# Cross-attention on one core: statistics two pairs ahead in a shared bank, squares on ScalarE, normalisation as two tensor products

## The reference

```python
mu  = mean(x, axis=(1, 2)); var = var(x, axis=(1, 2))      # one pair of numbers a sample
xn  = (x - mu) * rsqrt(var + 1e-5) * gamma + beta
q   = Wq xn + bq;  k, v = split(Wkv ctx + bkv)             # 8 heads of 64
att = softmax(q k^T / 8)                                   # 256 x 256 for each head and sample
out = x + Wo concat(att v) + bo
```

## Time and profile before

| | us |
|---|---|
| median of 3 runs | 746.16 (744.21 to 749.26) |
| the profiled execution | 746.77 |
| its span, first to last instruction | 744.9 |
| busy in it: PE, DVE, ACT, POOL | 675.6, 690.6, 623.1, 579.6 |
| granted TensorE clock, mean | 0.998 |

### The profile page before, as it was taken

How to read it: one execution, slowest core, us unless ns; L and a number is a source line. 1 busy time by engine, 2 the same in 40 slices (tenths; PEclk the granted TensorE clock), 3 DMA queues, 4 the chain that set the end, 5 groups by cost and what they waited for, 6 DMA issues and landing times.

```text
span 744.9 us, 29909 instructions
## 1 busy us (share of the span) xinstructions
PE 675.6 (91%) x11204; PEld 447.4 (60%) x11204; DVE 690.6 (93%) x1124; ACT 623.1 (84%) x2248; POOL 579.6 (78%) x360
## 2 busy tenths in 40 slices
PE   5889989999999999999999999999999999999986
PEld 4556566566666656666656666665666665666654
DVE  1589999999999999999999999999999999999993
ACT  2579888888988889888888998888988888898883
POOL 2477978777888777898877788877789888788873
PEclk9999999999999999999999999999999999999999
DMA  6022222222222222222222221222221222222111
GB/s 120 19 53 74 53 59 72 70 69 74 64 55 62 69 67 70 78 50 59 67 69 68 75 69 45 68 68 68 70 78 51 58 67 69 73 76 58 45 44 32
DMA packets 74814, 47.56 MB, mean 64 GB/s; under 512 B 33748, under 2 KB 74708, under 8 KB 74772
## 3 DMA queue, kind: packets, MB, share of 16 engines
q1 hardware_dynamic: 72848, 46.59, 23.6%
q10 hardware_dynamic: 1924, 0.40, 0.3%
HBM read 25.96 MB, written 4.19 MB: 40 GB/s over the span
## 4 chain that ended last, share of the span: by engine, by line
PE 57%; DVE 23%; issue 12%; ACT 4%; SPq 2%; DMA 1%; DVEq 0%; ACTq 0%
PE z L400 32%; PE fill L366 20%; DVE neg_max L537 9%; DVE probs_t L550 8%; ACT probs L482 3%; PE z L411 3%; DVE squared L580 3%; SPq L291 1%; DMA wv<-in_L_xattn_Wkv 1%; DVE recip L543 1%; DVE y L593 1%; PE z L421 1%; DVE variance L586 1%; DMA x<-in_x 1%; PE z L378 1%
## 5 line engine op out<-in xcount | busy, mean ns | idle before, releaser
L638 POOL TENSOR_TENSOR probs<-probs,recip 128x1024 f32<-128x1024 f32 x256 | 482.0, 1892 | 131.3 <-DVE recip L543 127.1
L482 ACT ACTIVATE probs<-fill,neg_max 128x256 f32<-128x256 f32 x1024 | 473.2, 484 | 92.1 <-DVE neg_max L537 88.8
L537 DVE TENSOR_REDUCE neg_max<-fill 128x4 f32<-128x1024 f32 x256 | 306.7, 1208 | 15.5 <-PE fill L366 15.2
L366 PE MATMUL fill<-c,t 64*128 64x256 f32 x2048 | 289.1, 407 | 32.0 <-ACT probs L482 28.6
L550 DVE STREAM_TRANSPOSE probs_t<-probs 128x1024 f32<-128x1024 f32 x256 | 311.5, 1222 | 0.8 <-POOL probs L638 0.8
L400 PE MATMUL z<-probs_t,ctx_keys 32*64 32x256 f32 x8192 | 254.4, 381 | 12.2 <-DVE variance L586 10.9
L366 PEld LDWEIGHTS fill<-c,t 64*128 64x128 f32 x2048 | 183.2, 190 | 125.4 <-ACT probs L482 95.7
L400 PEld LDWEIGHTS z<-probs_t,ctx_keys 32*64 32x64 f32 x8192 | 176.5, 131 | 77.2 <-issue 35.7
L482 ACT ACTIVATION_READ_ACCUMULATOR probs<-fill,neg_max 128x1 f32 x1024 | 221.7, 216 | 0.0
L491 ACT ACTIVATE t<-z,d_col 128x512 f32<-128x512 f32 x128 | 88.5, 741 | 7.1 <-PE z L378 7.0
L652 POOL TENSOR_SCALAR xhat<-x,mean,rstd 128x256 f32<-128x256 f32 x64 | 78.1, 1221 | 0.1
(11 more groups left out here) (38 smaller groups left out, 109.8 us busy)
## 6 DMA issues: line engine op xcount, KB each, us to landing
ctx_keys<-ctx_turned SPq DMA_DIRECT2D x512, 32.0 KB, 1.8
x<-in_x SPq DMA_DIRECT2D x64, 128.0 KB, 2.7
c<-in_ctx SPq DMA_DIRECT2D x64, 128.0 KB, 2.7
ctx_rows<-in_ctx SPq DMA_DIRECT2D x128, 32.0 KB, 1.7
x_res<-in_x SPq DMA_DIRECT2D x32, 128.0 KB, 2.1
out<-y SPq DMA_DIRECT2D x32, 128.0 KB, 1.7
wq<-in_L_xattn_Wq ACTq DMA_DIRECT2D x2, 128.0 KB
wv<-in_L_xattn_Wkv SPq DMA_DIRECT2D x2, 128.0 KB
```

What stands on the lines that cost most here:

```text
L366: mm = pe.matmul(banks[:, o, K * qt:K * qt + K], t[p][r:r + 64, hp, s, 128 * qt:128 * qt + 128], c2[p][r:r + 64, s, :], start=True, stop=True)
L482: ins = act.activation(probs[:, k % SLOTS, g, :], bank[:, K * qt:K * qt + K], ACT.Exp, bias=neg_max[:, k, g:g + 1], accum_out=denom[:, k, ...
L537: dve.tensor_reduce(neg_max[:, k, :], fill[k % PAIRS_OF_BANKS][:, :, :].rearrange("p o (t k) -> p (o t) k", t=QT), AX.X, ALU.max, negate=T ...
L638: pool.tensor_tensor(p, p, recip[:, k, :].unsqueeze(2).broadcast_to([128, 2 * QT, K]), ALU.mult).then_inc(probs_ready, 1)
```

## The change

The statistics are computed earlier and in other pieces. The channel moments belong to the pair three ahead, the mean to the pair two ahead, the variance to the pair ahead. `channel_spread` becomes `centre` (DVE) and `squares` (ACT: each of two columns times itself by the scale operand); PE adds squares and channel variances by two matmul calls into one sum. POOL subtracts the mean from both samples at once in place, and later multiplies both by the inverse root. `mean_var` and `mean` have two buffers. All five order tables are new. The diff without the new buffers' declarations and the branches that call the new functions:

```diff
-PE_ORDER = (at('scores', 0.00, 1.12, 3.45, 4.98, 7.20, 10.10, 10.87, 13.52)
-            + at('mix', 18.00, 18.76, 20.22, 21.75, 22.51, 23.96, 24.73, 25.42) + at('project_out', 30.21)
-            + at('project_in', -4.44, -3.75) + at('mean', -16.22) + at('var', -15.24))
-ACT_ORDER = (at('exp', 1.93, 3.39, 5.57, 7.31, 9.13, 12.04, 13.84, 15.63) + at('t', -2.59, -0.79, 1.00, 1.43)
-             + at('z', 26.50, 27.24))
-DVE_ORDER = (at('weights', -2.64, 0.96) + at('max', 0.98, 2.44, 4.61, 6.36, 8.18, 11.09, 11.92, 14.52)
-             + at('recip', 4.28, 6.30, 8.04, 9.87, 10.78, 13.60, 15.35, 18.38)
-             + at('turn', 7.19, 9.01, 9.93, 12.75, 13.66, 15.41, 19.42, 21.45) + at('moments', -30.11)
-             + at('mean_var', -28.73) + at('spread', -15.74) + at('sample_var', -14.19)
-             + at('turn_context', 4.34) + at('result', 32.64))
-POOL_ORDER = (at('divide', 5.51, 6.92, 8.33, 10.63, 12.04, 13.80, 15.54, 18.58) + at('root', -12.01)
-              + at('norm', -10.47, -6.26))
-SYNC_ORDER = (at('load_x', -5.06) + at('load_c', 14.52) + at('load_ct', 5.14) + at('spread_context', 4.94)
-              + at('residual', 24.64) + at('store', 33.14))
+PE_ORDER = (at('scores', 0.00, 1.50, 3.83, 5.37, 7.58, 10.49, 11.25, 13.91)
+            + at('mix', 18.38, 19.14, 20.59, 22.13, 22.90, 24.35, 25.11, 25.80) + at('project_out', 30.59)
+            + at('project_in', -4.06, -3.37) + at('mean', -31.26) + at('var', -15.24))
+ACT_ORDER = (at('exp', 2.24, 3.89, 6.01, 7.76, 9.52, 12.42, 14.22, 16.01) + at('t', -2.21, -0.41, 1.38, 1.81)
+             + at('z', 26.89, 27.62) + at('square', -22.87))
+DVE_ORDER = (at('weights', -2.26, 1.34) + at('max', 0.98, 2.93, 5.05, 6.81, 8.56, 11.47, 12.87, 14.81)
+             + at('recip', 4.99, 6.75, 8.50, 9.40, 12.81, 14.74, 15.70, 19.77)
+             + at('turn', 7.64, 9.46, 10.35, 13.88, 15.76, 18.07, 20.13, 21.89) + at('moments', -35.70)
+             + at('mean_var', -34.29) + at('centre', -30.20) + at('sample_var', -14.18)
+             + at('turn_context', 3.83) + at('result', 32.62))
+POOL_ORDER = (at('divide', 6.07, 7.47, 8.88, 10.29, 13.01, 14.93, 17.03, 19.96) + at('root', -13.56)
+              + at('norm', -15.66, -10.63))
+SYNC_ORDER = (at('load_x', -9.43) + at('load_c', 14.91) + at('load_ct', 4.63) + at('spread_context', 4.43)
+              + at('residual', 24.62) + at('store', 33.12))
...
                     if kind == "load_x" and owner.shift(2).exists():
-                        wait(sync, xhat_ready, owner.count(PS, PS))
+                        wait(sync, xhat_ready, owner.count(1, 1))
                         load_x(owner.shift(2), rows[kind])
...
+                    if pair.shift(3).exists():
+                        wait(pe, centred_ready, pair.shift(3).count(2, 2))
...
             def sum_means(pair):
                 wait(pe, mean_var_ready, pair.count(PS, PS))
                 if pair.shift(-1).exists():
-                    wait(pe, t_ready, pair.shift(-1).count(HP, 2))
+                    wait(pe, centred_ready, pair.shift(-1).count(2, 2))
+                if pair.shift(-2).exists():
+                    wait(pe, variance_ready, pair.shift(-2).count(1, 1))
+                    wait(pe, t_ready, pair.shift(-2).count(HP, 2))
+                pe.matmul(z[:, 1, 0:PS], ones[:, :], mean_var[pair.parity()][:, :, 0], start=True, stop=True
+                          ).then_inc(mean_summed, 1)
+
+            def sum_spreads(pair):
+                wait(pe, squared_ready, pair.count(PS, PS))
                 if pair.shift(-1).exists():
                     wait(pe, variance_ready, pair.shift(-1).count(1, 1))
-                pe.matmul(z[:, 1, 0:PS], ones[:, :], mean_var[:, :, 0], start=True, stop=True).then_inc(mean_summed, 1)
-
-            def sum_spreads(pair):
-                wait(pe, spread_ready, pair.count(1, 1))
-                pe.matmul(z[:, 1, PS:2 * PS], ones[:, :], spread[:, :], start=True, stop=True).then_inc(var_summed, 1)
+                    wait(pe, t_ready, pair.shift(-1).count(HP, 2))
+                pe.matmul(z[:, 1, PS:2 * PS], ones[:, :], squared[:, :], start=True, stop=False)
+                pe.matmul(z[:, 1, PS:2 * PS], ones[:, :], mean_var[pair.parity()][:, :, 1], start=False, stop=True
+                          ).then_inc(var_summed, 1)
...
+            def squares(pair):
+                wait(act, centred_ready, pair.count(2, 2))
+                for s in range(PS):
+                    act.activation(squared[:, s:s + 1], centred[:, s:s + 1], ACT.Identity, scale=centred[:, s:s + 1]
+                                   ).then_inc(squared_ready, 1)
...
-            def channel_spread(pair):
+            def centre(pair):
+                p = pair.parity()
                 wait(dve, mean_summed, pair.count(1, 1))
                 if pair.shift(-1).exists():
-                    wait(dve, xhat_ready, pair.shift(-1).count(PS, PS))
-                dve.tensor_copy(mean[:, :], z[:, 1, 0:PS]).then_inc(centred_ready, 1)
-                dve.tensor_tensor(centred[:, :], mean_var[:, :, 0], z[:, 1, 0:PS], ALU.subtract
+                    wait(dve, var_summed, pair.shift(-1).count(1, 1))
+                if pair.shift(-2).exists():
+                    wait(dve, xhat_ready, pair.shift(-2).count(1, 1))
+                dve.tensor_copy(mean[p][:, :], z[:, 1, 0:PS]).then_inc(centred_ready, 1)
+                dve.tensor_tensor(centred[:, :], mean_var[p][:, :, 0], z[:, 1, 0:PS], ALU.subtract
                                   ).then_inc(centred_ready, 1)
-                wait(dve, centred_ready, pair.count(2, 2))
-                dve.tensor_tensor(squared[:, :], centred[:, :], centred[:, :], ALU.mult).then_inc(squared_ready, 1)
-                wait(dve, squared_ready, pair.count(1, 1))
-                dve.tensor_tensor(spread[:, :], squared[:, :], mean_var[:, :, 1], ALU.add).then_inc(spread_ready, 1)
...
             def inverse_root(pair):
-
                 wait(pool, variance_ready, pair.count(1, 1))
-                wait(pool, x_loaded[pair.parity()], pair.dma_count(1) * 2)
                 if pair.shift(-1).exists():
-                    wait(pool, xhat_ready, pair.shift(-1).count(PS, PS))
+                    wait(pool, xhat_ready, pair.shift(-1).count(1, 1))
+                pool.tensor_tensor(rstd[:, :], variance[:, :], minus_half[:, :], ALU.pow).then_inc(rstd_ready, 1)
+
+            def subtract_mean(pair):
+                p = pair.parity()
+                wait(pool, centred_ready, pair.count(2, 2))
+                wait(pool, x_loaded[p], pair.dma_count(1) * 2)
+                pool.tensor_tensor(x2[p][:, :, :], x2[p][:, :, :], mean[p][:, :].unsqueeze(2).broadcast_to([128, PS, S]),
+                                   ALU.subtract).then_inc(x_centred, 1)
+
+            def normalise(pair):
+                p = pair.parity()
+                wait(pool, x_centred, pair.count(1, 1))
+                wait(pool, rstd_ready, pair.count(1, 1))
+                if pair.shift(-1).exists():
                     wait(pool, projected, pair.shift(-1).count(HP // 2, HP // 2))
-                pool.tensor_tensor(rstd[:, :], variance[:, :], minus_half[:, :], ALU.pow).then_inc(rstd_ready, 1)
-
-            def normalise(pair, s):
-                p = pair.parity()
-                pool.tensor_scalar(xhat[:, s, :], x2[p][:, s, :], mean[:, s:s + 1], rstd[:, s:s + 1],
-                                   ALU.subtract, ALU.mult).then_inc(xhat_ready, 1)
+                pool.tensor_tensor(xhat[:, :, :], x2[p][:, :, :], rstd[:, :].unsqueeze(2).broadcast_to([128, PS, S]),
+                                   ALU.mult).then_inc(xhat_ready, 1)
```

More of the change, by code:

```diff
@@ L162, in build @@
         moments = sb("moments", [128, PS, 6])
-        mean_var = sb("mean_var", [128, PS, 2])
-        mean = sb("mean", [128, PS])
+        mean_var = [sb(f"mean_var_{i}", [128, PS, 2]) for i in range(2)]
+        mean = [sb(f"mean_{i}", [128, PS]) for i in range(2)]
         centred = sb("centred", [128, PS])
         squared = sb("squared", [128, PS])
-        spread = sb("spread", [128, PS])
         variance = sb("variance", [128, PS])
@@ L201, in build @@
         squared_ready = sem("squared_ready")
-        spread_ready = sem("spread_ready")
         var_summed = sem("var_summed")
@@ L205, in build @@
         rstd_ready = sem("rstd_ready")
+        x_centred = sem("x_centred")
         xhat_ready = sem("xhat_ready")
@@ L371, in project_in @@
                 if i == 0:
-                    wait(pe, xhat_ready, pair.count(PS, PS))
+                    wait(pe, xhat_ready, pair.count(1, 1))
                 if pair.shift(-2).exists():
@@ L511, in steps @@
                         exponentials(owner, item)
+                    elif kind == "square":
+                        squares(owner)
                     else:
@@ L569, in channel_mean_var @@
                 for s in range(PS):
-                    dve.bn_aggr(mean_var[:, s, :], moments[:, s, :]).then_inc(mean_var_ready, 1)
```

(22 more changed lines are left out.)

## The result

| | before | changed |
|---|---|---|
| median of 6 runs, us | 746.25 | 915.33 (911.07 to 918.78) |
| ratio | | 1.226, 95% interval 1.222 to 1.231 |
| profiled execution, its span, us | 746.77, 744.9 | 918.57, 916.8 |
| granted TensorE clock, mean | 0.998 | 0.879 |

What follows compares the result with a forecast made beforehand. DVE was taken to set the pace, PE close behind; after the change DVE waits on SP's queue for x. Start 37.2, 28 periods of 26.7 (747.6), 101.3 after, 1.9 around: 888 us, range 868 to 935.

Steps and rivals of the forecast that it cites:

- first project_in starts: PE's start: waiting for the early statistics and later loads, project_in begins near 22.6 us in place of 14.87.
- first context turn: DVE's first turn_context, delayed by the later start and the extra matmul, from 28.86 to about 37.2 us.
- SP's leg: From turn_context's end to x in place: 12.49 us of queue, 0.75 to second issue, 2.9 to land; 16.1 us.
- moments to the turn's end: DVE's work from x's landing to the next turn_context's end, with nothing else late: 10.6 us.
- period: Distance between successive pairs' context turns: 10.6 + 16.1 = 26.7 us against 22.02.
- last turn of 28 to the end: From pair 28's context turn to the end: 95.6 us before, plus one last stall of 5.7, makes 101.3.
- rival D: At the moments of P+3: x is there in time, 21.4 us a pair, 736 us; chance 0.06.
- the likeliest case: DVE stalls for x behind SP's queue, clock at full speed: 888 us; chance 0.53.
- Rival B: PE's idle time during the stall lowers the clock: 1.1 us more a period, 919 us; chance 0.30.
- the stall: DVE reaches moments before x has landed and stands still 5.7 us, from P = 0 to P = 28.
- ACT's squares: Two 128x1 squares on ACT at 0.25 us each, 0.5 a pair (0.4 to 1.0), hidden in idle time.
- POOL's products: POOL's normalisation as two tensor_tensor over 512, about 0.95 us each, 1.9 in all; worth nothing on the path.

Runs made afterwards that it cites:

- Experiments 1: Changed kernel with load_x moved ahead of the four load_ct transfers in SP's order, behind spread_context; 833.01 us, 1.114 to the kernel before.
- Experiment 2: Changed kernel with load_x moved ahead of spread_context in SP's order; 796.63 us, 1.067 to the kernel before.
- experiment 3: Changed kernel with load_x ahead of spread_context and the residual's load ahead of both in SP's order; 735.63 us, 0.985 to the kernel before.
- experiment 5: Changed kernel with project_out's sixteen matmul calls done three times in all but the last pairs; 891.13 us, 1.193 to the kernel before.
- experiment 4: Changed kernel with DVE's moments moved after the pair's last turn and mean_var behind the result; 819.30 us, 1.097 to the kernel before.
- experiment 7: Kernel before with squared and spread formed by one DVE tensor_scalar per sample instead of two tensor_tensor; 731.84 us, 0.980.

## Why the prediction was right, and where it was short

The prediction's steps, in the changed kernel's profiled execution:

| step | forecast, us | measured, us |
|---|---|---|
| first project_in starts | 22.6 | 22.56 |
| first context turn | 37.2 | 36.48 |
| turn's end to moments (SP's leg) | 16.1 | 16.25 in the pair shown, 16.52 as a mean of 28 |
| moments to the turn's end | 10.6 | 11.4 with the clock down, 10.45 without, 11.13 as a mean of 28 |
| period | 26.7 | 27.65 |
| last turn of 28 to the end | 101.3 | 106.2 |
| span | 886.1 | 916.8 |

**Right, and shown:** the place, the reason and the price of SP's leg. Experiments 1, 2 and 3 take it away in steps (period 27.65, 24.68, 23.54, 21.44), and the last brings the time that rival D named. The start was right to 0.1 us for project_in. The forecast's 37.2 for the first context turn is 0.3 us more than its own terms give (28.86 + 7.73 + 0.35 = 36.9).

**Short by 30.7 us of span**: 26.5 in the 28 periods (774.1 against 747.6), 4.9 after them, 0.7 less at the start. Two terms of the period were mis-sized. The second leg, 10.6 us, measured 11.13: in the likeliest case the forecast kept the clock at full speed, and with it up the leg measures 10.24 to 10.45, so the clock is the whole of this error and a little more. SP's leg, 16.1 us, measured 16.52: in most pairs it was 16.0 to 16.6, but 17.4 to 18.9 in pairs 1 to 4 and 18.1 in pair 27, where the issues were dearer than in the pair from which the forecast took them. Rival B is what happened: it forecast 1.1 us a pair more and an idle PE of 4.7 us; with PE kept busy 0.84 us came back (experiment 5), and the idle time was 3.44 us. Its sum, 919, came close to the profiled 918.57 with some luck, since it knew nothing of the dearer issues and of the tail. I gave it 0.30 beside 0.53; the trace of before had one fall, after a stretch with PE busy for 1.56 of 4 us, and the stall made sparser ones (0.95 us busy from 416 to 420), with a fall in every pair. Weighing the tail's 2.43 us of idleness against it was the mistake. The Trainium skill, TensorE: Matmul & The Clock Gate, section Why this matters for your kernels, spoke for B with its warning of idle gaps, and the trace agrees for the gap of 3.44 us.

**SP's dearer issues.** In pairs 1 to 4, and from 27 on, the same sixteen issues take longer, in some of these pairs the four of `load_ct` too:

```profile
782.37 11.11 SPq L290 DMA_DIRECT2D ctx_keys<-ctx_turned  x16
...
811.04 11.05 SPq L290 DMA_DIRECT2D ctx_keys<-ctx_turned  x16
822.14 2.59 SPq L253 DMA_DIRECT2D ctx_rows<-in_ctx  x4
```

11.05 and 2.59 us in place of 10.13 and 1.95. Most of the sixteen still follow each other at 0.63 us; one of them takes 1.57 (at 817.36), and one of the four 1.16. The kernel before has that too (11.60 at 76.51), but there it was hidden. Pairs 0 to 2 and those from 27 on are written out, and 3 and 4 are the loop's first pass; but pair 0 was at 10.09 us. What makes these issues dear wasn't tried.

**The 4.9 us after the periods** are SP's only in part. The last context turn is at 882.83 and the end 33.97 us later; before, the turn is at 713.51 and the end 31.39 later. These 2.6 us stand in the kernel of experiment 3 as well, where SP's order is mended:

```profile
700.93 0.41 DVE L576 STREAM_TRANSPOSE ctx_turned<-ctx_rows 128x256 f32<-128x256 f32 x1
```

Its span ends at 734.9, again 33.97 us later. So SP's queue is not their cause; they come with the new orders, in which the context's turn also has another place. The forecast counted nothing for the orders there, and which entry makes the difference wasn't tried. The other 2.3 us lie between the turns of pairs 28 and 31, among them SP's dearer issues in pair 28, 1.2 us over its forecast leg.

**Small steps.** The stall was forecast at 5.7 us and shows as 4.25 or 2.6: PE's slowed steps had already delayed DVE inside the leg, which rival B counted as covered by the slack. ACT's squares take 0.48 us a pair (forecast 0.5), POOL's products 1.04 us each (0.95). PE's third call of the statistics takes 0.36 us from start to end at full clock and, as the calls overlap, adds about 0.25 (forecast 0.35). In the stalled pairs none of them is on the path.

**Where one rival's condition was incomplete:** D said that x in time would do. Experiment 2 had x in time and 797 us; the residual's load had to be in time too. Any reordering of SP's table moves everything behind it, and the forecast looked at `load_x` alone.

## What to carry to other kernels

An order table without the cost of issuing is blind to one engine: here sixteen small transfers keep SP for 10 us, and a consumer moved to within 10.4 us of them stood still, though DVE itself got less to do (676.3 against 690.6 us). For each transfer that is moved, add up the issues ahead of it on its queue, its landing, and the work that its reader has until then; then do the same for every transfer that it pushes back. And where a stall idles PE for microseconds in every pair, price the clock's fall into the likeliest case.

## What the runs showed of the hardware

- More matmuls made the kernel faster: 3.6 us of extra PE work a pair in the idle stretch, 24.2 us less in all; scores went from 2.08 back to 1.13 us (experiment 5).
- The length of one gap did not tell whether the clock would fall. It fell to 0.50 behind an idle PE of 1.27 us (experiment 4, 419 us) and behind two gaps of 1.80 and 0.64 us (changed kernel, ahead of 447.86 and 450.39), while 2.43 us near the end of the kernel before, after ten microseconds of a PE that was never idle, left it at 1.00.
- A 128x2 `tensor_tensor` on DVE takes 0.16, 0.72 or 0.76 us, by what POOL is doing; the `tensor_scalar` of experiment 7, which does square and sum for one column, takes 0.264 to 0.275 us in all its 64 places.
- The sixteen issues of 32 KB on SP followed each other at 0.63 us (10.13 us in all); in the pairs at either end single ones of them took 1.2 to 1.7 us, which makes 11 to 12 us in all.
